# Masked attention in one kernel: projections of three blocks a step later, stores of factor halves earlier in SyncE's order, a tile of values inside a unit of scores

## The reference, cut to what matters

```
h = relu(layernorm(x))                      # x: 4096 x 512
q, k, v = h @ Wq.T + bq, key @ Wk.T + bk, value @ Wv.T + bv
s = (q @ k.T) / 64 * adj                    # 4096 x 4096
s = where(|s| < 1e-5, -1e9, s)
out = x + (softmax(s) @ v) @ Wm.T + bm
```

## Time and profile before

| | us |
|---|---|
| median of three runs | 1569.11 |
| the profiled execution's own time | 1568.17 |
| its span, first to last instruction | 1566.3 |
| TensorE busy in the span | 1529.0 (98%) |
| VectorE busy | 1144.7 (73%) |
| ScalarE busy | 634.6 (41%) |
| mean granted TensorE clock | 0.999 |

### The profile page before, as it was taken

How to read it: one execution, slowest core, us unless ns; L and a number is a source line. 1 busy time by engine, 2 the same in 40 slices (tenths; PEclk the granted TensorE clock), 3 DMA queues, 4 the chain that set the end, 5 groups by cost and what they waited for, 6 DMA issues and landing times.

```text
span 1566.3 us, 24291 instructions
## 1 busy us (share of the span) xinstructions
PE 1529.0 (98%) x7062; PEld 699.4 (45%) x7062; DVE 1144.7 (73%) x2539; ACT 634.6 (41%) x1036; POOL 211.8 (14%) x279
## 2 busy tenths in 40 slices
PE   8998999998999999999999999999999999999998
PEld 5543443443444444444444444444444444444444
DVE  5989877786868777686777768677776867777562
ACT  5776333333433333343333334333333433333342
POOL 5162000001010200201020020102002010200100
PEclk9999999999999999999999999999999999999999
DMA  9834776668858777685877768587776858778674
GB/s 343 275 78 98 172 175 146 154 169 221 213 143 216 174 190 185 167 214 141 216 172 187 188 167 214 141 216 174 192 182 167 214 141 215 174 189 188 152 162 108
DMA packets 459509, 283.25 MB, mean 181 GB/s; under 512 B 377411, under 2 KB 385859, under 8 KB 459334
## 3 DMA queue, kind: packets, MB, share of 16 engines
q1 hardware_dynamic: 459456, 282.67, 71.7%
q10 hardware_dynamic: 6, 0.01, 0.0%
HBM read 175.38 MB, written 15.73 MB: 122 GB/s over the span
## 4 chain that ended last, share of the span: by engine, by line
PE 76%; DVE 9%; DMA 5%; issue 4%; ACT 3%; SPq 2%; ACTq 0%; DVEq 0%
PE R L777 12%; PE R L778 12%; PE R L779 12%; PE S L777 9%; PE S L779 9%; PE S L778 9%; PE M L777 3%; PE M L778 3%; PE M L779 3%; DMA key_factors<-early 2%; DVE Zbuf L1567 1%; DVE Zbuf L1519 1%; DVE drop L1621 1%; DMA ho<-row 1%; PE R L894 1%
## 5 line engine op out<-in xcount | busy, mean ns | idle before, releaser
L1223 ACT ACTIVATE drop<-Zbuf 128x512 f32<-128x512 f32 x256 | 161.0, 629 | 684.9 <-DVE cmx L1519 537.9
L777 PE MATMUL R<-Vbuf,pT 128*128 128x512 f16 x1008 | 382.1, 379 | 8.5 <-DMA pT<-ph 4.6
L779 PE MATMUL R<-Vbuf,pT 128*128 128x512 f16 x1008 | 382.0, 379 | 0.0
L778 PE MATMUL R<-Vbuf,pT 128*128 128x512 f16 x1008 | 382.0, 379 | 0.0
L777 PE MATMUL S<-Kbuf,qT 128*128 128x512 f16 x738 | 279.8, 379 | 5.5 <-ACT Zbuf L1190 5.5
L779 PE MATMUL S<-Kbuf,qT 128*128 128x512 f16 x738 | 279.7, 379 | 0.0
L778 PE MATMUL S<-Kbuf,qT 128*128 128x512 f16 x738 | 279.7, 379 | 0.0
L1567 DVE SCALAR_TENSOR_TENSOR Zbuf<-S,rs,adjb 128x512 f32<-128x512 f32 x178 | 133.2, 748 | 116.3 <-PE S L779 110.5
L1519 DVE CUSTOM_DVE_ANT_0 Zbuf<-drop,Zbuf 128x512 f32<-128x512 f32 x256 | 178.8, 698 | 0.0
L1621 DVE TENSOR_SCALAR drop<-drop,rs 128x512 f32<-128x512 f32 x256 | 145.8, 570 | 23.0 <-ACT drop L1223 19.8
L1229 ACT ACTIVATE Zbuf<-Zbuf,smx 128x1024 f32<-128x1024 f32 x128 | 157.5, 1230 | 5.4 <-DVE smx L1533 2.5
(11 more groups left out here) (251 smaller groups left out, 1886.8 us busy)
## 6 DMA issues: line engine op xcount, KB each, us to landing
Kbuf<-key_factors SPq DMA_DIRECT2D x134, 512.0 KB, 4.2
adjb<-in_adj_dram SPq DMA_DIRECT2D x256, 256.0 KB, 2.9
xq<-in_x_dram SPq DMA_DIRECT2D x32, 256.0 KB, 2.8
Kbuf<-in_L_gnn_key_dram SPq DMA_DIRECT2D x8, 1024.0 KB, 13.5
xr<-in_x_dram SPq DMA_DIRECT2D x32, 256.0 KB, 2.8
out_dram<-xr SPq DMA_DIRECT2D x31, 256.0 KB, 4.3
Vbuf<-in_L_gnn_value_dram SPq DMA_DIRECT2D x7, 1024.0 KB, 7.3
key_factors<-early SPq DMA_DIRECT2D x32, 128.0 KB, 2.6
```

Of the source, the lines that this page charges most:

```text
L777: nc.tensor.matmul(ps, lhs[0], rhs[0], start=start, stop=False, skip_group_check=added)
L778: nc.tensor.matmul(ps, lhs[0], rhs[1], start=False, stop=False, skip_group_check=added)
L779: return nc.tensor.matmul(ps, lhs[1], rhs[0], start=False, stop=stop, skip_group_check=added)
L1223: nc.scalar.activation(drop[:, :], tile_of(s.i, s.j), ACT.Abs).then_inc(abs_ready, 1)
```

## The change

Three edits. `HEAD` gets entries for blocks 4, 5 and 6 and holds up to step 41: their projections are in steps 24, 32 and 40 in place of 23, 31 and 39; block 4's `scaled` is in step 24 in place of 28, block 5's `halves_q` in step 33 in place of 32; the rest of them stays where the rule had it. The store of a factor's half is taken from behind the output's transpose, the query's transpose and the loads of x in SyncE's step, and put right behind the probabilities' transpose. The third product of a unit's first step is taken from behind the second, and put behind the first tile of values of that step.

```diff
-        HEAD = {1: (1, 2, 3, 4, 4, 5), 2: (8, 9, 10, 11, 11, 12), 3: (14, 15, 16, 17, 17, 18)}
+        HEAD = {1: (1, 2, 3, 4, 4, 5), 2: (8, 9, 10, 11, 11, 12), 3: (14, 15, 16, 17, 17, 18),
+                4: (21, 22, 23, 24, 24, 25), 5: (29, 30, 31, 32, 32, 33), 6: (37, 38, 39, 40, None, 41)}
...
-                    if fixed and self.t < 21:
+                    if fixed and self.t < 42:
...
                         .then_inc(pT_spare[u % 2] if spare(turn) else pT_in[u % 2], 16)
+                if s.making is not None:
+                    if s.making >= 0:
+                        (w, t, part), half = PIECES[s.making // 2], s.making % 2
+                        dst = kt[FACTORS.index((w, t)), :, :].rearrange("p (h s n) -> p h s n", h=2, s=2)
+                        sp.wait_ge(kt_lo, s.making + 1)
+                        sp.dma_start(dst[:, :, part, half * 256:(half + 1) * 256], tb[:, :, :]).then_inc(kt_stored, 16)
                 if s.c == 4 and s.has_out and not last_out(s):
...
-                    if s.making >= 0:
-                        ... (the same lines, at the end of the block on s.making)
...
                         unit_product(W[0], qS[:, :, 2:4, :], 2 * s.w + 1, True).then_inc(unit_mm, 1)
-                        wait(pe, kr_in[4], 64 * s.nth + 16 * (s.w + 1))
-                        wait(pe, p1_ready, NU * s.nth + s.w + 1)
-                        unit_product(S[s.j % 2], qT[:, 0, :, 2:4, :], 4, False).then_inc(scores_done, 1)
...
                     for m in range(CM):
+                        if s.unit == 0 and m == 1:
+                            wait(pe, kr_in[4], 64 * s.nth + 16 * (s.w + 1))
+                            wait(pe, p1_ready, NU * s.nth + s.w + 1)
+                            unit_product(S[s.j % 2], qT[:, 0, :, 2:4, :], 4, False).then_inc(scores_done, 1)
```

## The result

| | before | changed |
|---|---|---|
| median, us | 1569.35 (4 runs, 1568.63 to 1570.76) | 1550.49 (4 runs, 1550.15 to 1550.67) |
| profiled execution, own time | 1568.17 | 1550.67 |
| its span | 1566.3 | 1548.9 |

The ratio is 0.9879, 95% interval 0.9861 to 0.9896: 18.9 us faster. Predicted were 1551.4 for the median, and 1548.6 for the span (1566.3 less 17.7). The medians differ by more than the profiled executions (18.9 against 17.5), since the kernel before's profiled execution was 1.2 faster than its median.

A forecast was written before the change was run, and what follows sets the result against it. TensorE's own stream and its wait for ScalarE's copy bound the steady passes, factor-making gaps the stretch before. Tile 7.47, projections 7.73 and stores 2.47 sum to 17.7 us: 1550.5 profiled, 1551.4 median, range 1548.5 to 1556.

The forecast's parts named there:

- The tile's sum of 7.47: Unit's third product: 0.585 us won in each of passes 4 to 14, 0.38 in the last, 0.65 in the first.
- VectorE's crowded step: Step 24, where the moved scales meet a factor sum: about 9 us from 191.2, ending about 200.5, costed at nothing.
- The stores edit: 2.47, bounds 0 to 4.7: Sooner factor stores: 0.77 us before step 47's projection, 1.7 of the 3.89 at the end of the making.
- the gaps of 0.77, 1.60 and 2.28: TensorE stalls before step 47's projection and at 359.00 and 365.18, the only ones credited to the stores edit.
- my 206: Step 25: the store is issued at about 206, some 3 us sooner than 209.49.
- what the sooner stores win for TensorE is only what still stalls: Stores edit: credits only step 47's gap and the two at the end of the making, 2.47 us.
- their 7.73: Projections edit: 5.55 us of stalls in steps 23, 31, 39, 1.65 slow clock, 0.53 gap at 263; bounds 4 and 7.9.
- my first rival: Steps 19 to 52: removed stalls are given back later, only the unit's 7.5 us is left, 1561.6; chance 0.10.
- TensorE would be at 355.0: Start of the first unit's second product, 365.18 less the stalls expected to go before it.
- The copy is the last wait: Step 4; its rival: third product waits as long for factor or copy, 7.5 us not won, 1558.9; chance 0.08.
- The slower clock: Rival: one more PSUM bank change drops the clock in each of 13 passes, 1.65 us each, 1573; chance 0.03.

The follow-up runs named there:

- the pair: Kernel before with the projections' and the stores' edits, without the tile; measured 1558.80 us, ratio 0.9927, 11.1 us gained.

## Why the prediction was right, and where it was not

**The time, and the tile.** 17.7 was worked out, 17.4 came in the spans and 18.9 in the medians. The priced stalls came out nearly one by one. The tile's sum of 7.47 holds: the unit's stalls in passes 4 to 14 and in the last are gone, and in the first pass 0.17 is left (0.82 less 0.65 was forecast). It measured 6.7 alone and 8.3 on top. Other stalls from 372 to 1500 went from about 2.3 to 1.55.

**The projections.** All that I had priced went: no stall in steps 23, 31, 39 or at 263, and clock 1.00 around 240. VectorE's crowded step ran from 192.33 to 202.24. It began 1.1 later than I had it and ended 1.7 later than my 200.5; one small instruction in it took 1.26, where such take 0.15 to 0.22. TensorE did not stand for it: it stood nowhere from 174 to 353.

**The step that failed: "The stores edit: 2.47, bounds 0 to 4.7".** Booked as the prediction booked it, behind the projections, the term is near: the gaps of 0.77, 1.60 and 2.28 are 0, 0 and 2.12 in the changed kernel, so 2.5 went, and the pair is 11.1 - 8.3 = 2.8 above the projections alone. Its split was off: the first of the last two gaps went whole and the second hardly at all. Where the store goes out and why ScalarE goes on sooner was right too (issued at 205.67 for my 206; ScalarE at 208.20 in place of 212.72, with 2.85 idle in place of 5.51). What failed is 4.7 as the most that this edit can be worth: it measured 7.4 alone, and 5.8 (5.0 by the gains) on top of both others. The rule behind it, "what the sooner stores win for TensorE is only what still stalls", gives a share in one order of booking. I had given steps 23 and 31 to the projections first, and did not see two things:

- The stores alone take away step 31's 3.16 with its slow clock. A late row transpose has two cures, an earlier one or a later use, and I had priced the second only. Nor had I priced the stores behind a base factor's store or a load of x, of which step 24's puts ScalarE 3 us ahead.
- The projections alone don't keep all of their 7.73. In that kernel the three later gaps grew from 0.77, 1.60 and 2.28 to 1.40, 2.57 and 1.91, which gives 1.2 back. As I read it, TensorE arrives earlier at the end of a making whose pace the stores set: my first rival, in small, and the stores' edit keeps it off. Without the stores (and with the tile) the last two are 1.98 and 2.38, with a slow clock behind (1.65); with them 0 and 2.12. With step 47's 0.94 that is 4.8 of the 5.8. The rest is a balance of stalls that vary between executions: step 21's was 1.6 smaller without the stores, and those from 372 to 1500 added up to some 3 more.

So the sum came right because it counts step 31's stall once. It did not know what each edit is worth: on top of the others the projections add 5.6 less than booked, and the stores 3.3 more (6.2 and 2.5 by the gains).

That TensorE would be at 355.0 was right but for one thing: the changed kernel's start is 356.15, and step 21 had a stall of 1.76 where before it was 0.62, behind a query's transpose that took 2.45 to issue. In another execution of the changed kernel that transpose took 1.23, the stall is 0.48 and the start 354.9.

**The rivals.** The copy is the last wait, by 13 stalls that went, and twice over. The slower clock did not come: one more change of bank, and the steady pass has a clock of 1.00 and matmuls 0.2155 apart. The Trainium skill, "TensorE: Matmul & The Clock Gate", "A second HAM failure mode: psum-queue depth-cycling", tells of a kernel that cycles through banks and idles briefly between its groups of matmuls, and whose clock goes up and down. The steady pass has the changes of bank, some after only three or six matmuls, but not the idle time, and its clock stays up.

## What to carry to other kernels

If two edits attack one late chain, one making the producer earlier and the other the consumer later, price each alone and together: the stall counts once, and an order of booking decides which edit seems worthless. A store that another engine's next write waits for belongs ahead of the transposes (1.2 us each to issue here), loads and larger stores in its queue, and its head start was passed on for six steps here. Where an engine waits for a copy by a small fixed amount, one tile of independent work in between can pay the whole of it; here three tiles cost 0.29 a pass elsewhere.

## What the runs showed of the hardware

Not every stall brings the slow clock, and the limit is not sharp. From step 17 on, the clock fell behind stalls of 3.35, 3.17, 3.16, 2.97, 2.92 and 2.69, and also behind 2.38 (in three kernels), 2.20 and 2.13; it stayed up behind 2.57 (the projections alone, at 353.5), 2.28, 2.24, 2.16, 2.12 and 2.01. Here the kernel without the tile, behind a stall of 2.13 in step 52:

```profile
356.90:360.00 3.10, 2.90 (x8) 0.85 (x7) 1.35 (x2) 1.61 (x3) 0.00 (x0) 0.50 0.76 213
```

That is the lower level (1.2 GHz), and matmuls 0.42 apart in place of 0.2155: some eight of them, 1.65 us each time. The Trainium skill, "TensorE: Matmul & The Clock Gate", "What's actually happening", ties the clock to how busy TensorE has just been. The traces agree: these falls all stand behind stalls of over 2 us. So a stall of 2.1 to 2.6 us carries a chance of 1.65 more, and some of the spread comes from it. The kernel before ran from 1566.15 to 1573.21 in 17 runs; the fastest has a mean granted clock of 1.000 and the two slowest 0.997, and 0.003 of 1570 us is 4.7 of the 7. It is not all: the changed kernel ran from 1550.15 to 1550.67 in four runs and up to 1554.51 once in five, and the clock was 1.000 in that one as well.
